# Rotary sums behind a slot's maxima, and a unit's row maxima sent one slot sooner, in a fused MoE-attention-MoE kernel

## The reference

```python
x = x + 0.5 * ffn(layernorm(x))
x = x + attn(layernorm(x))
x = x + 0.5 * ffn(layernorm(x))

# attn: 16 query heads, 4 key/value heads, head dimension 16
q = q * cos + rotate_half(q) * sin
k = k * cos + rotate_half(k) * sin
attn = softmax(q @ k.T * scaling);  out = (attn @ v) @ Wo.T

# ffn: 32 experts, inner width 96, top 8 kept until their share reaches 0.8
for each expert: acc += (silu(x @ Wg.T) * (x @ Wu.T)) @ Wd.T * combine[:, e]
```

## Time and profile before

| | us |
|---|---|
| median of three runs | 2269.64 (2267.43 to 2271.03) |
| time of the profiled execution | 2266.18 |
| its span, first to last instruction | 2264.4 |
| PE busy in it | 2201.2 (97%) |
| DVE busy | 1597.2 (71%) |
| ACT busy | 1173.5 (52%) |
| POOL busy | 1094.3 (48%) |

### The profile page before, as it was taken

One profiled execution on the slowest core, in us unless ns is written; L12 is line 12 of the kernel. 1 busy time (PEld: TensorE's weight loads), 2 busy tenths in 40 slices (PEclk: granted clock), 3 DMA queues, 4 the chain that ended last, 5 costly groups with the idle time before them and its releaser, 6 DMA issues.

```text
span 2264.4 us, 47194 instructions
## 1 busy us (share of the span) xinstructions
PE 2201.2 (97%) x18794; PEld 1487.3 (66%) x18794; DVE 1597.2 (71%) x3139; ACT 1173.5 (52%) x1925; POOL 1094.3 (48%) x956
## 2 busy tenths in 40 slices
PE   3999999999999999999999999999999999999998
PEld 2888875565566565565566566666666666688887
DVE  8756679787887877877877876777777754444543
ACT  4433331566656556556556666665666656433332
POOL 1767654354444444544434443444444344466665
PEclk9999999999999999999999999999999999999999
DMA  5211121011111120111201110010110010101010
GB/s 223 81 42 36 40 58 30 20 45 32 35 31 41 25 61 24 36 37 31 48 25 46 27 50 23 20 43 18 24 52 13 20 30 20 30 27 41 21 39 20
DMA packets 157957, 88.51 MB, mean 39 GB/s; under 512 B 103588, under 2 KB 149924, under 8 KB 156968
## 3 DMA queue, kind: packets, MB, share of 16 engines
q1 hardware_dynamic: 157592, 85.45, 14.0%
q10 hardware_dynamic: 144, 0.03, 0.0%
HBM read 63.14 MB, written 11.80 MB: 33 GB/s over the span
## 4 chain that ended last, share of the span: by engine, by line
PE 91%; DVE 6%; POOL 1%; issue 1%; DMA 1%; ACT 0%; SPq 0%; POOLq 0%; DVEq 0%
PE PS L1262 44%; PE PS L1283 22%; PE PS L1295 11%; PE PS L1328 10%; DVE arena L1003 2%; PE PS L1244 1%; PE PS L1357 1%; PE PS L1307 1%; DVE arena L980 1%; DVE arena L988 1%; POOL arena L611 1%; POOL arena L616 0%; PE PS L1230 0%; DVE parts L1096 0%; DVE arena L970 0%
## 5 line engine op out<-in xcount | busy, mean ns | idle before, releaser
L1262 PE MATMUL PS<-XT,WGU 128*128 128x256 f16 x9216 | 1112.3, 273 | 5.6 <-DVE arena L980 2.3
L1262 PEld LDWEIGHTS PS<-XT,WGU 128*128 128x128 f16 x9216 | 875.9, 98 | 223.6 <-issue 121.2
L616 POOL TENSOR_TENSOR arena<-arena 128x512 f16<-128x512 f32 x384 | 450.8, 1174 | 1059.8 <-ACT arena L695 1059.8
L1003 DVE TENSOR_REDUCE arena<-PS 128x1 f32<-128x512 f32 x1024 | 657.3, 684 | 299.9 <-PE PS L1295 295.3
L711 ACT ACTIVATE arena<-PS,fac 128x512 f32<-128x512 f32 x1024 | 646.3, 684 | 263.7 <-PE PS L1307 263.2
L688 ACT ACTIVATE arena<-PS,fac 128x512 f32<-128x512 f32 x384 | 263.8, 687 | 758.3 <-PE PS L1262 758.3
L1283 PE MATMUL PS<-WD,arena 128*128 128x256 f16 x4608 | 572.8, 274 | 2.6 <-POOL arena L616 2.4
L611 POOL TENSOR_TENSOR arena<-arena 128x512 f32<-128x512 f32 x384 | 501.5, 1306 | 72.8 <-DVE arena L988 68.7
L1283 PEld LDWEIGHTS PS<-WD,arena 128*128 128x128 f16 x4608 | 430.8, 98 | 151.4 <-issue 95.5
L980 DVE SCALAR_TENSOR_TENSOR arena<-arena,PS 128x512 f32<-128x512 f32 x384 | 261.1, 680 | 253.2 <-ACT arena L688 252.2
L1295 PE MATMUL PS<-arena 48*128 48x512 f16 x1024 | 318.8, 382 | 18.2 <-DVE arena L1003 13.5
(11 more groups left out here) (119 smaller groups left out, 732.2 us busy)
## 6 DMA issues: line engine op xcount, KB each, us to landing
arena<-ce_scratch SPq DMA_DIRECT2D x256, 128.0 KB, 3.2
arena<-wgu SPq DMA_DIRECT2D x4, 1536.0 KB, 13.0
arena<-q_scratch SPq DMA_DIRECT2D x192, 32.0 KB
arena<-ktab_c SPq DMA_DIRECT2D x16, 256.0 KB, 3.7
q_scratch<-arena SPq DMA_DIRECT2D x32, 128.0 KB, 1.8
out<-X SPq DMA_DIRECT2D x8, 512.0 KB, 3.0
X<-wd SPq DMA_DIRECT2D x2, 1536.0 KB, 23.1
X<-x SPq DMA_DIRECT2D x1, 3072.0 KB, 11.7
```

The costliest lines, as they stand in the source:

```text
L616: pool.tensor_tensor(hs[1][:, d % HS, :], tw[d % 2], hs[0][:, d % HS, :], ALU.subtract).then_inc(lo_done, 1)
L1003: dve.tensor_reduce(mx[:, half * REP * QT + c:half * REP * QT + c + 1], PS[:, B_MAX + half, :], AX_X, ALU.max).then_inc(max_taken, 1)
L1262: ins = pe.matmul(PS[:, b, j * HALF_G:(j + 1) * HALF_G], WGU[w][:, kt, part * CHUNKS + c + j, :], XT[r][:, k % 2, kt, half * HALF_G:(half ...
```

## The change

`rope_sum` moves on DVE from just behind `product` to behind the maxima of the second and third visits. `turn_max_rows` follows it, and is made in step R + 1 instead of R + 2. `max_rows_low` stays in step R + 1 on POOL but moves ahead of `rope_low`, `weigh` and the norm's pieces, to just behind `low`. `rows` on SP goes from step R + 2 to R + 1. No instruction is added or removed.

```diff
@@ sync: -570,7
-                    if d == ROWS_AT[u] + 2:
+                    if d == ROWS_AT[u] + 1:
                         rows(u)
@@ gpsimd: -637,6
                 if 0 <= d < SLOTS:
                     low(d)
+                if d - 1 in ROWS_AT:
+                    max_rows_low(ROWS_AT.index(d - 1))
                 if s - 2 in join_slots(k):
                     rope_low(k - 1, join_slots(k).index(s - 2))
                 if d + 1 < SLOTS:
...
-                if d - 1 in ROWS_AT:
-                    max_rows_low(ROWS_AT.index(d - 1))
                 if d in OUT_AT:
                     outputs_split(OUT_AT.index(d))
@@ vector: -1147,8
                 if (d, 0) in VISIT:
                     unit_ends(VISIT[d, 0])
-                if s - 1 in join_slots(k):
-                    rope_sum(k - 1, join_slots(k).index(s - 1))
...
                 if (d, 2) in VISIT:
                     unit_ends(VISIT[d, 1])
                     visit(VISIT[d, 2])
-                if d - 2 in ROWS_AT:
-                    turn_max_rows(ROWS_AT.index(d - 2))
+                if s - 1 in join_slots(k):
+                    rope_sum(k - 1, join_slots(k).index(s - 1))
+                if d - 1 in ROWS_AT:
+                    turn_max_rows(ROWS_AT.index(d - 1))
                 if d in OUT_AT:
                     normalise(OUT_AT.index(d))
```

## The result

The changed kernel takes 2256.52 us (median of 5 runs, 2256.33 to 2256.85), the kernel before 2268.08 us (5 runs, 2266.34 to 2271.03). The ratio is 0.9947 with a 95% interval of 0.9933 to 0.996: 11.6 us faster by the medians (the ratio is that of the means). Between the two profiled executions it is 2266.18 - 2256.52 = 9.66 us. Two numbers stand out: the difference of the medians is 1.9 us larger than that of the profiles, and the runs of the kernel before spread over 4.7 us where those of the changed kernel lie within 0.5.

What follows compares the result with a forecast made beforehand. PE bounds the kernel, busy 2201 of 2264 us, so only its idle time can change. Gains of 4.4 (rows), 0 (subtraction and turn) and 5.0 (sum) make 9.4 us: 2256.8 like the profiled execution, median 2260.2, range 2254 to 2267.

Steps and rivals of the forecast that it cites:

- part 3: Rotary sum on DVE behind the maxima: shorter sums and fewer PE waits give 5.0 us, between 0 and about 11.
- Part 1: First unit's row maxima, slot 77: the 3.3 us wait and its clock loss go, 4.4 us gained, at most 5.0.
- The rival in which the rows come no sooner: Landing or queue holds the first unit's rows, not the turn; only the sum's gain stays: 2264.6 us, chance 0.06.
- Part 2: POOL's subtraction and DVE's turn in their new places: 0 us, bounded by 0.2 us of waiting in each unit.
- the slower rival: DVE's new wait for POOL in step R + 1 of all units passes to PE: 2279 us, chance 0.05.
- 131: Two-visit slot: the sum escapes weigh and shortens from 1.69 to near 0.7 us, 0.9 us on PE.
- the 6 that I had named as a sign: Sign of being right: PE's `max_taken` waits for DVE's maxima fall from 13.5 to about 6 us.
- Slots 83 and 203: Maxima ahead of the sum remove PE's 1.63 us waits; gains limited by DVE's slack: 1.35 and 1.1 us.
- Slot 107: Two-visit slot: the moved sum starts as weigh is ending and so runs shorter, 0.6 us on PE.
- the other course that part 3 names and sets aside: Moved sum still meets weigh in 14 two-visit slots, up to 1.0 us of DVE each; gains in 107 and 131 would be 0.
- Slot 155: Not named; among the 12 other slots said to have no PE wait behind the sum: 0 us.
- the clock rival: The clock drop behind the first unit's 3.3 us wait is not always met, 1.5 us less gain: 2261.7 us, chance 0.08.

Runs made afterwards that it cites:

- e2: Kernel before with only the rotary sum moved; turn, subtraction and rows in their old places: 2260.99 us.
- e3: Changed kernel with SP's rows left in step R + 2: 2256.67 us in one run.
- e11: Changed kernel with turn and rows a slot sooner for the first unit alone, the 15 others at the old distance: 2256.31 us.
- e4: Changed kernel with POOL's subtraction for the row maxima behind weigh of the same step instead of behind low: 2256.82 us.
- e9: Changed kernel with the rotary sum back right behind the product in slots 83 and 203 alone: 2261.25 us.
- e5: Changed kernel with the rotary sum moved only in the four slots with three visits, in its old place elsewhere: 2257.24 us.
- e7: Changed kernel with DVE turning the values ahead of the rotary sum in a group's first piece: 2255.74 us.
- e1: Kernel before with only the first unit's rows chain made sooner; the rotary sum stays in its old place: 2263.31 us.

## Why the prediction was right, and where it was off

**Sign and size between profiles: right.** 9.4 us forecast, 9.66 found. All instructions are the same; PE's waits changed, and 1.8 us of its busy time with the clock. That the sum is right to 0.3 us is partly luck: see part 3.

**Part 1, the first unit's rows: right.** 4.4 forecast, 4.6 found. The read back began at 394.08 and PE did not stop. PE's own matmuls, laid over each other, tell the wait from what follows it. The lead rises by 3.4 us at the first matmul behind the wait (402.89 in the kernel before, 399.83 in the changed one), and by another 1.3 us in the 4.3 us behind it, where the kernel before ran at the lower clock; 0.1 is lost again by 412. The clock had cost an estimated 1.7 us there, so 0.4 us of it came back as PE's waits for the maxima, where I had said 0.6. That the drop was met in every execution is inferred: both profiled executions with the wait show it, the five runs of e2 agree within 0.4 us, and none of the 48 runs of the kernel before is lower than 2266.2, where one without the drop would be. The rival in which the rows come no sooner falls; so does the claim that SP's step matters (e3).

**Part 2: right, with a wait where none was counted.** DVE's turn waits only in the last unit. The turn itself (0.235 us), now in step 204, costs 0.13 us at slot 206 (e11); I had costed that at nothing, and looked for it in slot 132 when I wrote e11. e4 bounds the slower rival: even with POOL's subtraction behind `weigh` it is 0.3 us by the medians and 0.5 by the lead, not 19. Its step that fails is that a wait of DVE passes to PE: of nine such waits one did.

**Part 3: the sum of the terms right by luck, most terms off.** 5.0 was forecast and 5.2 found, but slots 83, 203 and 131 gave 1.3 us more than their terms (131 0.3 of it), and slots 107 and 155 1.1 less. The errors cancel. The waits for the maxima fell to 8.1 us and not to the 6 that I had named as a sign.
- *Slots 83 and 203* were undersized (2.45 forecast, 3.4 found). I took back from PE whatever exceeded DVE's slack at the next join. In the changed kernel PE shows no wait for DVE of 0.2 us or more in slots 84 to 86; one pair of score halves starts 0.41 us apart instead of 0.22. Behind 203 the slack was less, and 0.4 us did come back.
- *Slot 107* was oversized (0.6 forecast, 0 found). The step "it starts when `weigh` (0.16 us behind `product`, 1.27 long) is within 0.15 us of its end" failed. In 107 POOL is still at `low`, `weigh` begins 0.6 us behind `product`, and the sum took 1.33 us again. The term was drawn from slot 131, where the sum had met `weigh`. In 107 it had met `low`, as it had in 14 of the 18 slots. This row of the kernel before lies beside the sum of the earlier trace rows, which ends at 608.82, 0.54 us behind it:

```profile
607.12 1.16 POOL L616 TENSOR_TENSOR arena<-arena 128x512 f16<-128x512 f32 x1 [5.97 <-ACT arena L695]
```

  The move traded `low` for `weigh`: in the changed kernel 10 of the 14 sums in slots with two visits still end 0.54 to 0.55 us behind the end of a `weigh`. So the other course that part 3 names and sets aside, that the moved sum still meets `weigh`, came true in most slots, and with it a gain of 0 in 107; for 131, where 1.2 us was won, it did not. The median of the sum's length fell to 0.855 us, not to 0.7. The view of its line in the changed kernel:

```profile
L970 DVE TENSOR_TENSOR arena<-arena,turned x24: 649/855/1336, 186.9 to 1283.9; 128x512 f32<-128x512 f32 x16, 64x512 f32<-64x512 f32 x8
```

- *Slot 155* was missing (-0.5). I counted what the sum delays and not which idle time it filled.

**The median: 2260.2 forecast, 2256.5 found, inside the range but 3.7 us off.** With the five runs of the kernel before in place of three, its median is 2268.08, and the gain by the medians is 11.6 us against the 9.4 forecast. The step that failed is the sentence "the median is 3.46 us higher and I carry that difference over". The offset comes from waits in the kernel, those in slots 83 and 203 above all (e9), behind which the clock falls in some executions. The profiled execution of before had escaped both. Where they are taken away, the offset goes too: changed kernel, e2, e5 and e7 have medians within 0.1 us of their profiled executions. I had the clock rival at the wrong wait. The drop behind the 3.3 us one was there in every execution as far as the runs tell, the drops behind the 1.6 us ones only now and then. A drop behind a 1.6 us wait was seen in one profiled execution, of e1 in slot 203; that slot 83 does the same is inferred from the levels of e9.

What stays open: what lifts some runs of the kernel before to 2270.6 us and more, and the slots of e1's levels one by one, since only one execution of e1 was profiled.

## What to carry to other kernels

On the engine that sets the end, look at how an instruction of a busy helper engine lies to what PE wants next: a sum and a turn, 1.9 us together, ahead of a 1.3 us pair of maxima cost 1.6 us of waiting and, now and then, the same again in clock. Moving it behind is worth little where it used to run in a gap of its own engine, so read the idle time in front of the neighbours as well as the waits behind. When a kernel's runs fall on levels and one profiled execution is of the lowest, look for a wait of PE that may or may not lower the clock, and don't add the offset of the median to a forecast that removes that wait.

## What was not expected of the hardware

- Two waits of the same length (1.62 and 1.63 us) at the same place in the same stream of work: granted clock 1.00 behind the one and 0.68 behind the other. The levels of the runs of e1 and e9 lie 1.5 to 1.7 us apart.
- A sum that starts while POOL is in `low` or `weigh` ends 0.54 to 0.55 us behind the end of POOL's instruction, whenever the sum began (37 cases in the profiled executions of the two kernels), and it works the other way too: a `weigh` that starts beside a sum took 1.64 to 1.74 us in the kernel before, one that is there first 1.27. The values' turn, with one input, took 0.71 us in all 8 places.
